# Conditioned attention block on one core: scores in 32-row tiles, feed-forward by half blocks, a reordered beginning

## The reference

```python
x = (x - mean) * rsqrt(var + 1e-5) * w + b          # LayerNorm over 256 features
x = (x + tanh(cond @ lin_w.T + lin_b)) * w + b
h = gamma_a * rms(x) + beta_a                        # gamma, beta, alpha: rows of cond @ weight
q, k, v = split(h @ W_q.T), split(h @ W_k.T), split(h @ W_v.T)   # 16 heads of 16
p = softmax(0.25 * q @ k.T)                          # per sequence and head, 64 x 64
x = x + alpha_a * ((p @ v) @ W_o.T)
h = gamma_f * rms(x) + beta_f
x = x + alpha_f * ((silu(h @ gate.T) * (h @ hidden.T)) @ out_w.T + out_b)
```

## Time and profile before

| | before |
|---|---|
| median of 3 runs (lowest, highest) | 1082.89 us (1080.6, 1084.52) |
| profiled execution, its own time | 1082.04 us |
| its span, first to last instruction | 1080.1 us |
| PE busy | 1015.9 us, 94% |
| PE weight loads (beside matmuls) | 848.0 us, 79% |
| DVE, ACT, POOL busy | 687.5, 646.9, 565.1 us (64%, 60%, 52%) |
| DMA, share of 16 engines | 6.6% |
| granted TensorE clock, mean | 0.988 of 2.4 GHz |

### The profile page before, as it was taken

How to read it: one execution, slowest core, us unless ns; L and a number is a source line. 1 busy time by engine, 2 the same in 40 slices (tenths; PEclk the granted TensorE clock), 3 DMA queues, 4 the chain that set the end, 5 groups by cost and what they waited for, 6 DMA issues and landing times.

```text
span 1080.1 us, 21896 instructions
## 1 busy us (share of the span) xinstructions
PE 1015.9 (94%) x7964; PEld 848.0 (79%) x7964; DVE 687.5 (64%) x1278; ACT 646.9 (60%) x1742; POOL 565.1 (52%) x535
## 2 busy tenths in 40 slices
PE   3768899999999999999999999999999999999997
PEld 3757788888888888888888888888888888887775
DVE  4478666766676676667667666766666665655554
ACT  2455666665666666666666666666666666665322
POOL 3667846555564645556464555646455564333310
PEclk9889999999999999999999999999999999999999
DMA  5100000010101001010100101010010000000000
GB/s 176 58 21 21 2 21 2 1 40 2 41 1 37 5 2 40 2 41 1 33 9 2 40 2 41 2 33 8 2 40 21 2 17 5 2 21 2 20 20 19
DMA packets 16760, 22.91 MB, mean 21 GB/s; under 512 B 1168, under 2 KB 12048, under 8 KB 16656
## 3 DMA queue, kind: packets, MB, share of 16 engines
q1 hardware_dynamic: 16656, 21.54, 6.1%
HBM read 13.15 MB, written 8.39 MB: 20 GB/s over the span
## 4 chain that ended last, share of the span: by engine, by line
PE 51%; DVE 18%; ACT 16%; issue 13%; POOL 1%; DMA 1%; DVEq 0%; ACTq 0%; POOLq 0%; SPq 0%
PE psum L253 14%; PE psum L255 12%; PE psum L254 12%; DVE least L511 4%; ACT v_diag L737 4%; ACT probs L750 4%; PE psum L361 4%; ACT prod_hi L777 3%; DVE row_sum L524 3%; DVE late L584 3%; PE psum L385 2%; PE psum L373 2%; DVE normed_f L551 2%; ACT tanh L771 2%; DVE xf_lo L569 1%
## 5 line engine op out<-in xcount | busy, mean ns | idle before, releaser
L750 ACT ACTIVATE probs<-psum,least 128x64 f32<-128x64 f32 x904 | 197.2, 330 | 126.3 <-DVE least L511 126.3
L904 POOL TENSOR_TENSOR probs<-probs,inv_sum 128x512 f32<-128x512 f32 x128 | 134.2, 1049 | 259.7 <-DVE inv_sum L529 259.7
L576 DVE SCALAR_TENSOR_TENSOR late<-tanh,psum 128x512 f32<-128x512 f32 x128 | 88.1, 688 | 227.4 <-ACT tanh L771 227.4
L253 PE MATMUL psum<-xf_hi,ffn_hi 128*128 128x512 f32 x512 | 204.9, 400 | 9.4 <-DVE xf_lo L569 8.8
L254 PE MATMUL psum<-xf_lo,ffn_hi 128*128 128x512 f32 x512 | 202.2, 395 | 0.0
L255 PE MATMUL psum<-xf_hi,ffn_lo 128*128 128x512 f32 x512 | 202.1, 395 | 0.0
L590 DVE TENSOR_TENSOR prod_lo<-late,prod_hi 128x512 fp32r<-128x512 f32 x128 | 120.4, 941 | 97.4 <-ACT prod_hi L777 97.4
L777 ACT ACTIVATE prod_hi<-late 128x512 fp32r<-128x512 f32 x128 | 80.3, 627 | 158.4 <-DVE late L584 125.7
L253 PEld LDWEIGHTS psum<-xf_hi,ffn_hi 128*128 128x128 f32 x512 | 96.1, 188 | 30.9 <-DVE xf_lo L569 9.8
L255 PEld LDWEIGHTS psum<-xf_hi,ffn_lo 128*128 128x128 f32 x512 | 96.2, 188 | 23.4
L771 ACT ACTIVATE tanh<-psum 128x512 f32<-128x512 f32 x128 | 77.5, 605 | 56.7 <-PE psum L255 56.7
(11 more groups left out here) (100 smaller groups left out, 2172.8 us busy)
## 6 DMA issues: line engine op xcount, KB each, us to landing
xin<-x_dram SPq DMA_DIRECT2D x16, 512.0 KB, 4.0
out_t_dram<-x_res SPq DMA_DIRECT2D x32, 256.0 KB, 4.2
q_heads<-attn_w_dram SPq DMA_DIRECT2D x1, 1024.0 KB, 7.5
x_res<-gate_w_dram SPq DMA_DIRECT2D x1, 1024.0 KB, 10.4
late<-hidden_w_dram SPq DMA_DIRECT2D x1, 1024.0 KB, 11.2
x_res<-out_w_dram SPq DMA_DIRECT2D x1, 1024.0 KB, 5.3
k_heads<-mod_w_dram SPq DMA_DIRECT2D x1, 448.0 KB, 5.8
ident<-identity_dram SPq DMA_DIRECT2D x1, 64.0 KB, 4.9
```

The source lines that it names most:

```text
L253: pe.matmul(out, stat_hi, mov_hi, start=first, stop=False)
L750: op = act.activation(probs[g % 2][:, h * SEQ:(h + 1) * SEQ], scores[:, h // 4, h % 4], ACT.Exp, bias=least[g % 2][:, h:h + 1], scale=-1.0)
L904: pool.tensor_tensor(by_head, by_head, inv_sum[g % 2][:].unsqueeze(2).broadcast_to([P, 8, SEQ]), ALU.mult).then_inc(probs_made, 1)
```

## The change

It moves no arithmetic to the host, and the outputs are the same function. Its parts:

1. Scores: eight matmuls for a sequence in place of four, each with 32 rows, 64 stationary and 128 moving columns; the four row groups write to four banks (3 to 6), the two feature halves to the two halves of the partitions. Queries need no mask then and are written by one ACT copy (`queries_out`). The value products go to the upper columns of the same four banks, so they too wait until the scores of the sequence before have been read (`score_banks_free`).
2. Feed-forward by parts: a step is two hidden tiles of 128 for 256 tokens, 36 matmuls with 256 columns in place of 18 with 512. The down projection fits one bank; its first matmul of each part has 512 columns, of which 256 are zeros, to clear the other half. There are still 128 steps, beginning in slot 12 in place of 15. `gate_ffn`, `add_ffn` and the store go by parts.
3. PE order in a slot: turned probabilities, value products, scores, and only then the norm work. DVE does `find_least` ahead of `make_residual` and the norm work.
4. In one of four slots (j = 2) DVE centres the scores and ACT makes one exponential, as in the slots ahead of the feed-forward. The two splits into high parts on ACT move from j = 2 to j = 3.
5. The beginning: the constants are loaded ahead of the conditions; PE makes only the first two of seven modulations before it turns x, the others later; the normalised x of block 1 comes from DVE; the raw attention weights have a buffer of their own; the feed-forward weights are split in slots -1 to 10.

```diff
-FFN_AT = 15
+FFN_AT = 12
-SPLIT_AT = -3
+SPLIT_AT = -1
+QUAD = 32
...
+            def score_banks_free(s):
+                if is_seq(s - 1):
+                    pe.wait_ge(scores_read, s)
+                if s % PSEQ == 3 and is_part(s // PSEQ - 1):
+                    pe.wait_ge(att_lo_made, s // PSEQ)
...
-                for mt in range(KT):
-                    for half in range(2):
-                        rows = slice(half * HALF, (half + 1) * HALF)
-                        mm = pe.matmul(score_bank[half][:, mt * P:(mt + 1) * P], q_heads[rows, m % 2, mt, j],
-                                       k_heads[rows, m % 2, mt, j], start=True, stop=True)
+                for kt in range(KT):
+                    for r in range(4):
+                        rows = slice(r * QUAD, (r + 1) * QUAD)
+                        mm = pe.matmul(score_bank[r][kt * SEQ:(kt + 1) * SEQ, 0:2 * SEQ], q_heads[rows, m % 2, kt, j],
+                                       k_heads[rows, m % 2, kt, j], start=True, stop=True)
...
-                up(gate_bank, 0, f).then_inc(gate_mm, 1)
+                for u in range(2):
+                    mm = up(gate_bank[:, u * PART:(u + 1) * PART], 0, 2 * q + u, m)
+                mm.then_inc(gate_mm, 1)
...
+                        if q == 0 and mt == 0 and u == 0:
+                            pe.matmul(by_kt(y_bank), ffn_hi[:, 2, cols],
+                                      prod_hi[f % 2][:].rearrange("p (b c) -> p b c", b=3)[:, 0:3:2],
+                                      start=True, stop=False)
+                        else:
+                            pe.matmul(out, ffn_hi[:, 2, cols], hi, start=False, stop=False)
...
             pe.wait_ge(mod_loaded, 16 * 2)
-            modulation()
+            modulation(SHIFT, 2)
...
                     turn_probs(s - 2)
+                score_banks_free(s)
+                if is_seq(s - 3):
+                    times_values(s - 3)
+                if is_seq(s):
+                    score(s)
                 norm_bank_free(s)
...
         def wide(g):
-            return g < FFN_AT
+            return g < FFN_AT or g % PSEQ == 2
...
             def attended_hi(m):
+                g = PSEQ * (m + 1) + 2
                 act.wait_ge(attended, PSEQ * (m + 1))
+                if is_seq(g):
+                    act.wait_ge(scores_read if wide(g) else least_made, g + 1)
```

More of the change, by code:

```diff
@@ L236, in _ @@
                              w.rearrange("(k p) h -> p k h", p=P)).then_inc(ffn_loaded, 16)
[L237 to L241, removed]
+            for s in range(FIRST_SLOT, LAST_SLOT):
+                if s == SPLIT_AT + 4:
                     sp.wait_ge(ffn_lo_made, 4)
@@ L255, in three_pass, with modulation @@
                 return pe.matmul(out, stat_lo, mov_hi, start=False, stop=last)
-            def modulation():
-                for i in range(7 * KT):
+            def modulation(first, rows):
+                for i in range(first * KT, (first + rows) * KT):
                     row, kt = i // KT, i % KT
-                    mm = pe.matmul(bank[i // 4][:, (i % 4) * P:(i % 4 + 1) * P],
-                                   mod_stage[:, row * D + kt * P:row * D + (kt + 1) * P],
+                    mm = pe.matmul(mod_bank(i, P), mod_stage[:, row * D + kt * P:row * D + (kt + 1) * P],
                                    cond_sb[0:COND, 0:BATCH], start=True, stop=True)
@@ L669, in _ @@
                 if s == FIRST_SLOT:
-                    split_attention_weights()
-                if grp % 2 == 0 and 1 <= (grp + 4) // 2 < NBLK:
+                    split_attention_weights(WK)
+                if s == FIRST_SLOT + 1:
+                    split_attention_weights(WQ)
+                if s == FIRST_SLOT + 2:
+                    split_attention_weights(WV)
+                    split_attention_weights(WO)
+                if s == FIRST_SLOT + 3:
+                    for t in range(TILES):
+                        token_stats(1, t)
+                if s == FIRST_SLOT + 6:
+                    normalise_tokens(1)
+                if grp % 2 == 0 and 2 <= (grp + 4) // 2 < NBLK:
                     token_stats((grp + 4) // 2, j)
-                if is_tile(f):
+                if is_step(f):
                     activate(f)
@@ L726, in queries_out @@
                     act.wait_ge(scored, PSEQ * (m - 1))
-                heads_out(q_heads, m, 2).then_inc(q_out, 1)
+                act.activation(q_heads[:, m % 2].rearrange("p k s t -> p (k s t)"), work, ACT.Copy, scale=-SCALE
+                               ).then_inc(q_out, 1)
             def values_out(m):
@@ L749, in exponentials @@
                 for h in range(8):
-                    op = act.activation(probs[g % 2][:, h * SEQ:(h + 1) * SEQ], scores[:, h // 4, h % 4], ACT.Exp,
+                    op = act.activation(probs[g % 2][:, h * SEQ:(h + 1) * SEQ], scores[:, h // 2, h % 2], ACT.Exp,
                                         bias=least[g % 2][:, h:h + 1], scale=-1.0)
@@ L776, in product_hi @@
                     act.wait_ge(out_mm, f - 1)
[L777 removed]
+                act.activation(prod_hi[f % 2][:, 0:BLK], prod, ACT.Copy).then_inc(prod_hi_made, 1)
             def split_ffn_weights(c):
@@ L783, in split_ffn_weights, with mod_rows, split_attention_weights @@
                                scale=1.0 if c < 8 else 0.5).then_inc(ffn_hi_made, 1)
-            def grouped(g):
-                return w_hi[:, WQ:WK + 1].rearrange("p w k d -> p (w k d)").rearrange(
-                    "p (m g a c) -> p m g a c", g=2, a=2, c=2 * DH)[:, :, g]
-            def by_half(g):
-                return w_raw[:, 0:WV * KT * D].rearrange("p (m a g c) -> p m a g c", g=2, a=2, c=2 * DH)[:, :, :, g]
+            def mod_rows(rows, first):
+                width = (rows.stop - rows.start) * KT * P
+                act.activation(mod[:, rows].rearrange("p w k s -> p (w k s)"), mod_bank(first, width), ACT.Copy
+                               ).then_inc(mod_out, 1)
+            def split_attention_weights():
+                act.wait_ge(attn_loaded, 16)
+                for w in (WQ, WK, WV, WO):
+                    act.activation(split_cols(w_hi, w), raw_weight(w), ACT.Copy).then_inc(w_hi_made, 1)
             act.wait_ge(consts_set, 1)
```

349 lines of the change are left out of this document (178 added, 171 removed).

## The result

| | before | changed |
|---|---|---|
| median of the runs | 1083.24 us | 1048.37 us (1047.5 to 1049.14) |
| ratio, 95% interval | | 0.9681 (0.966 to 0.9701) |
| span of the profiled execution | 1080.1 us | 1046.0 us |

The change makes the kernel 3.2% faster. The forecast was 1022 us with a range of 1005 to 1046, so the sign was right and 26 us of the 60 did not come.

A forecast was written before the change was run, and what follows sets the result against it. The prediction took the PE stream to bound the steady stretch, and chains and waits the stretch before the feed-forward. Terms of -36+3+4-12-9+2-6-5-1 = -60 took the span from 1080.1 to 1020, giving 1022 us, range 1005 to 1046.

The forecast's parts named there:

- Scores: Score matmuls of each sequence: two rounds over eight tiles, 0.36 us in place of 0.64, 128 times, -36 us.
- (a): Scores only half packed, the two passes of one matmul starting in order: 0.48 us a sequence, 1036 us in all; chance 0.15.
- (b): No packing of the feature halves in the score matmuls, gain 0: 1058 us; chance 0.07.
- Feed-forward pace: Feed-forward steps: 36 matmuls of 256 columns take about as long as 18 of 512; +3 us over 128 steps.
- Zeros: Down projection: 256 more columns of zeros in each of 32 parts, 0.117 us each, +4 us.
- Rival (d): Weight loads set the feed-forward's pace, making the kernel slower than before, 1480 us at a pace of 0.22; chance 0.03.
- Stalls that go: PE waits: the gate's for xf_lo goes in 15 blocks, -12 us; turned x's for product shrinks in 13 slots, -9.
- New waits: Slots j = 2: the added centre delays scale_f to about 4.9 us, when the hidden product starts; +2 us, bounds 0 and +20.
- Rival (c): The centre's chain is longer than counted, holding the hidden product or tanh 0.7 us in 29 groups: 1042 us; chance 0.12.
- Beginning: Before the first scores: fewer modulations first, so turned x and the residual start earlier; -6 us, bounds -8 and 0.
- Three slots fewer: Slots 12 to 14: their attention work moves beside the feed-forward, which starts three slots earlier; -5 us, bounds -9 and 0.
- End: Last work on DVE and POOL: DVE's 1.41 us becomes some 0.9, POOL's two sums become one; -1 us.

## Why the prediction failed, step by step

The bound was read rightly: the steady stretch is the PE stream, and most terms can be checked against it.

**Scores**, forecast -36: the mechanism held (two rounds, eight tiles, the order of the loops of no matter), the second round starts at 0.16 and not at 0.11. The gain is 0.240 a sequence, 128 x 0.240 = -31. This term was mis-sized by 5 us. Rivals (a) and (b) are out.

**Feed-forward pace**, forecast +3: in the kernel before, halving two thirds of the matmuls cost 1.5 us, so some +2 for all. **Zeros**, +4: down takes 1.52 in place of 1.40 once in four slots, 0.12 x 32 = +4. Rival (d) is out.

**Stalls that go**, forecast -12 and -9: both are gone. The slot that took 8.06 takes 7.06, and the norm piece no longer waits (turned probabilities and norm together 1.83 before, 0.97 now). But "what is late next is the same product, by a tenth or two" named the wrong thing: in the same slots the next turned probabilities wait for the activation, 1.63 in place of 1.40 in down and some 0.1 in the pieces behind it, 14 times, 4 to 5 us. The chain in slot 68, ScalarE, then VectorE, then PE:

```profile
528.90 0.63 ACT L722 ACTIVATE squares_a<-x_res 128x512 f32<-128x512 f32 x1 [1.14 <-DVE x_res L539]
529.43 1.73 ACT L781 ACTIVATE probs<-psum,least 128x64 f32<-128x64 f32 x8
531.00 0.64 ACT L804 ACTIVATE tanh<-psum 128x512 f32<-128x512 f32 x1
...
531.68 0.69 DVE L615 SCALAR_TENSOR_TENSOR late<-tanh,psum 128x512 f32<-128x512 f32 x1 [2.82 <-ACT tanh L804]
...
532.51 0.63 PE L387 MATMUL psum<-ident,probs 128*128 128x128 f32 x4
```

The prediction saw it ("tanh comes some 0.7 later") and took it as covered by the 2.8 us of hidden and down, which left too little: tanh, the activation and two hand-overs had to fit in too. The run with the exponentials and the statistics moved removes it.

**New waits**, forecast +2, bound +20. This is the step that failed, and it is where most of the 26 us are. The prediction put scale_f's end at 4.9 us into the slot and the hidden product at 4.9. The first number was right (514.64 - 509.75 = 4.89). The second was not: 4.9 is where the hidden product starts in the kernel before (0.44 + 0.53 + 0.36 + 0.65 + 1.52 + 1.40 of the table), and the prediction did not take off the 0.28 by which its own first term makes the scores shorter. In the changed kernel it is due at 514.35 - 509.75 = 4.60. A wait of 0.3 with a restart costs 0.5 in each of 29 slots, and more in the last two of them: the slots j = 2 take 16 us more than with the two operations swapped. Rival (c), given 0.12, is what happened in its effect, with 16 us in slots j = 2 and 4 to 5 in slots j = 0 for its 20. Its reason, a chain longer than counted, holds only for tanh: the chain to scale_f was as long as counted, and its deadline was earlier. Slots j = 3 are 0.05 to 0.1 above the clean 7.01, another 2.

**Beginning**, forecast -6: the weights landed at 8.72 (forecast 9.1), and turned x starts at 10.72 (forecast 10.9):

```profile
8.72 2.07 PE L270 MATMUL psum<-probs,k_heads 64*128 64x128 f32 x8 [8.72 <-DMA k_heads<-mod_w_dram]
10.72 1.11 PE L293 MATMUL psum<-ident,xin 128*128 128x128 f32 x4
```

Slot 12 begins 9.6 us earlier. The run with the modulations first accounts for 5.8 of it; the other 3.8 weren't taken apart (the sum had 12 x 0.28 = 3.4 from the scores, but PE isn't the bound there). **Three slots fewer**, forecast -5: four slots were measured at 9.9, so three would be some 7 by proportion, and that figure takes in two slow first slots in either form (slots 16 and 17 of that run take 8.27 and 11.09). In the changed kernel slots 12 and 13 take 10.25 and 9.61 where slots 16 and 17 take 7.44 and 8.09. In slot 12 PE is idle 1.08 us for the residual ahead of the first hidden product and 1.93 for the activation. Slot 13 has a stretch at the lower of the two clocks: the granted clock is 0.50 (1.2 GHz) from 104.1 to 106.9, and 256 columns take 0.21 in place of 0.117. Slot 13 takes 8.10 in the profile of the run without the centre, where the clock stays at 1.00, so the clock is its whole excess of 1.5. The kernel before had such a stretch as well (0.58 from 110 to 113). No term of the sum held these 4 us; slots 15 and 16 of the kernel before, its first with feed-forward, are only 0.3 above their like. **End**, -1: 1046.0 - 1041.2 = 4.8 in place of 5.8.

Together: -31 + 2 + 4 - 12 - 11 + 5 (activation) + 16 (scale_f) + 2 - 6 - 5 + 4 (slots 12 and 13) - 1 = -33, measured -34 (the -5 for three slots is the forecast's own figure; nearer -7 would make it -35). With three queue orders corrected the same change reaches 1027 us, 5 above the forecast. That is what the scores lack; the other differences, +4 for slots 12 and 13 and some -5 for pace, stalls and new waits, nearly cancel, which is luck.

The order of norm work and scores was priced at the old wait alone, 9 to 11 us. It is worth 38. The kernel with half blocks and the old order has waits that the old kernel had not. A likely reason is VectorE's queue, which was written for scores that come early; no run restored that queue. What the trace of before showed was the price of that order in that kernel, not in this one.

## What to carry to other kernels

Where one engine's stream is the bound and the others run beside it with tenths of a microsecond to spare, shortening the stream moves every deadline forward: work out the slack of each wait in the new slot, not in the old one, and price a miss at the restart too (0.3 of idle cost 0.5 here). An operation that is added to a queue costs what stands behind it, so try the order of the queue before removing the operation: one swap of two operations was worth 15 us, removing the centre 7. A wait that is written ahead of work it doesn't concern holds that work too, and a list of waits that names no releaser is settled by the times: look for what ended just before. And an edit that shifts a stage by some slots can close a buffer's ring on itself; check who frees the buffer in which slot (137 us here).

## What the hardware showed

Sixteen float32 passes over eight tiles of 32 rows by 64 columns start in two rounds 0.16 us apart, and from the last start it is 0.20 until the next tile shape starts, whichever way the loops stand. The former eight passes over two tiles of 64 by 128 started in four rounds, the second 0.21 after the first and the others 0.11 apart, with the same 0.20 behind the last. Full-row weight loads, one for each 256 float32r columns, are hidden at a pace of 0.117 us, and 1536 more of them cost 1.5 us in all (0.1 to 2.8). After 0.28 us of idle time the first start is followed by the next only 0.20 later, in place of 0.12, so the wait cost 0.5.
